# New places in the turn for the 37 kinds of pieces of a software-pipelined tokens stage

## The reference, cut to what matters

```python
x = conv_layer(x, ...)                     # 1x1 conv, depthwise 3x3, 1x1 conv, each with batchnorm; + x
t = to_tokens(x)                           # (32, 3136, 96)
def attn(v):
    h = relu(bn1(v @ w1.T))                # (32, 3136, 192)
    X = fft(h, axis=tokens, norm='ortho')
    xr = relu(X.real * rd - X.imag * idg + rb)
    xi = relu(X.imag * rd + X.real * idg + ib)
    y = ifft(xr + 1j * xi, axis=tokens, norm='ortho').real
    return bn2(y @ w2.T)                   # (32, 3136, 96)
t = t + attn(layernorm(t))                 # layernorm over the 96 channels of a token
t = t + ffn(layernorm(t))                  # 96 -> 384 -> relu -> 96, operands rounded to fp8, sums to fp16
return from_tokens(t)
```

## Time and profile before

| | us |
|---|---|
| median of 3 runs | 5966.26 |
| lowest, highest | 5946.19, 5976.29 |
| the profiled execution | 5949.41 |
| its span, first to last instruction | 5947.6 |
| PE busy over the span | 5426.3 (91%) |
| DVE busy | 3628.5 (61%) |
| ACT busy | 3418.6 (57%) |
| POOL busy | 1708.1 (29%) |

### The profile page before, as it was taken

How to read it: one execution, slowest core, us unless ns; L and a number is a source line. 1 busy time by engine, 2 the same in 40 slices (tenths; PEclk the granted TensorE clock), 3 DMA queues, 4 the chain that set the end, 5 groups by cost and what they waited for, 6 DMA issues and landing times.

```text
span 5947.6 us, 161991 instructions
## 1 busy us (share of the span) xinstructions
PE 5426.3 (91%) x59604; PEld 3538.5 (59%) x59604; DVE 3628.5 (61%) x6670; ACT 3418.6 (57%) x5674; POOL 1708.1 (29%) x964
## 2 busy tenths in 40 slices
PE   4979999999999969999868999999999999999996
PEld 4956565555555534444356666666667666666663
DVE  1046666666666643333327787777777778777775
ACT  2445555555555546666446666666666666666652
POOL 0047676667666600000011111111111111111100
PEclk9989999999999989999969999999989999889986
DMA  3646666666666579999846655655655665565551
GB/s 82 155 119 163 164 158 159 163 151 162 162 161 164 138 250 334 341 334 332 266 128 164 170 156 156 170 160 157 167 161 160 165 169 154 157 168 152 157 134 43
DMA packets 553255, 1042.04 MB, mean 175 GB/s; under 512 B 178512, under 2 KB 347280, under 8 KB 535888
## 3 DMA queue, kind: packets, MB, share of 16 engines
q1 hardware_dynamic: 552512, 1031.93, 62.6%
HBM read 552.39 MB, written 478.94 MB: 173 GB/s over the span
## 4 chain that ended last, share of the span: by engine, by line
PE 34%; issue 7%; DMA 3%; ACT 2%; DVE 2%; POOL 1%; SPq 1%; ACTq 0%; POOLq 0%; DVEq 0%
PE bank_w L1327 6%; PE bank_s L1336 4%; PE bank_x L1282 4%; PE bank_o L1307 3%; PE bank_l L1237 3%; PE bank_c L1290 3%; PE bank_c L1291 2%; PE bank_o L1318 2%; PE bank_c L1297 2%; POOL onat L1527 1%; PE bank_l L1264 1%; PE bank_x L1279 1%; DMA d<-c_scratch 1%; PE bank_l L1225 1%; ACT h L1400 1%
## 5 line engine op out<-in xcount | busy, mean ns | idle before, releaser
L718 POOL TENSOR_TENSOR hlo<-h,hhi 128x1682 f16<-128x1682 f32 x288 | 977.0, 3392 | 522.6 <-DVE hhi L749 522.6
L733 DVE BATCH_NORM_STATS2 stats<-z 128x392 f32 (+1 forms) x1152 | 597.0, 560 | 592.4 <-ACT z L670 553.6
L1519 POOL TENSOR_TENSOR y<-zin,x_tok 96x448 f32<-96x448 f32 x224 | 263.2, 1175 | 2207.2 <-ACT zin L1475 2160.2
L680 ACT ACTIVATE h<-c1ps,s 128x1512 f32<-128x1512 f32 x288 | 465.0, 1615 | 748.2 <-PE c1ps L596 748.2
L888 PE MATMUL pps<-z2m,w3T 128*96 128x392 f32 x2048 | 707.6, 499 | 13.9 <-ACT z2m L865 13.9
L617 PE MATMUL dwps<-hhi,taps 64*64 64x392 f16 x13824 | 699.1, 334 | 0.3 <-issue 0.3
L617 PE MATMUL dwps<-hlo,taps 64*64 64x392 f16 x13824 | 690.8, 330 | 2.6 <-issue 2.6
L865 ACT ACTIVATE z2m<-z2m,s 128x784 f32<-128x784 f32 x512 | 491.0, 1029 | 253.1 <-DMA z2m<-z_scratch 253.0
L1527 POOL TENSOR_TENSOR onat<-tb,o 96x448 f32<-96x448 f32 x224 | 242.7, 1084 | 1143.4 <-DVE o L1586 1143.4
L888 PEld LDWEIGHTS pps<-z2m,w3T 128*96 128x96 f32 x2048 | 324.8, 164 | 387.2 <-issue 367.6
L617 PEld LDWEIGHTS dwps<-hlo,taps 64*64 64x64 f16 x13824 | 408.4, 107 | 188.9 <-issue 8.7
(11 more groups left out here) (218 smaller groups left out, 10110.4 us busy)
## 6 DMA issues: line engine op xcount, KB each, us to landing
z_scratch<-z SPq DMA_DIRECT2D x1152, 196.0 KB, 3.2
z2m<-z_scratch SPq DMA_DIRECT2D x128, 1568.0 KB, 19.6
a_scratch<-a SPq DMA_DIRECT2D x224, 384.0 KB, 2.8
bt<-a_scratch SPq DMA_DIRECT2D x96, 672.0 KB, 8.1
c_scratch<-cc SPq DMA_DIRECT2D x128, 336.0 KB, 4.2
d<-c_scratch SPq DMA_DIRECT2D x128, 336.0 KB, 4.4
xa<-in_x_dram SPq DMA_DIRECT2D x32, 1176.0 KB, 7.3
xin<-in_x_dram SPq DMA_DIRECT2D x32, 1176.0 KB, 8.3
```

The lines of the kernel that those rows point to most:

```text
L680: nc.scalar.activation(to, src, ACT.Relu, bias=s1[:, 1, u:u + 1], scale=s1[:, 0, u:u + 1]).then_inc(h_ready, 1)
L718: nc.gpsimd.tensor_tensor(to, h, hi, ALU.subtract).then_inc(lo_ready, 1)
L733: nc.vector.bn_stats(stats[:, i, v, at:at + 6], z2[:, v % 3, g, r, :]).then_inc(s_stat, 1)
```

## The change

The numbers of all 37 kinds in `PLACES` are others; nothing else in the kernel differs. The same instructions are issued, on the same engines and with the same waits. Two of the kinds:

```diff
@@ PLACES
- 'act_square1': (1674, 1957),
+ 'act_square1': (1766, 1978),
...
- 'row1': (2046, 2236),
+ 'row1': (2068, 2780),
```

More of the change, by code:

```diff
@@ new lines @@
+PLACES = {'load_in': (5, 73, 274, 393, 625, 703, 857),
+ 'act_bn3': (295, 451, 587, 745, 869, 999, 1157),
+ 'pool_y': (310, 500, 630, 782, 793, 1013, 1331),
+ 'store_t': (1149,),
+ 'act_square1': (1766, 1978),
+ 'mean1': (1872, 1994),
+ 'square1': (1876, 2014),
+ 'act_mean1': (1903, 2063),
+ 'dve_var1': (2037, 2148),
+ 'act_std1': (2013, 2138),
+ 'row1': (2068, 2780),
+ 'w1': (2210, 2258, 2309, 2388, 2535, 2687, 2749, 2849, 2903, 3005, 3111, 3208, 3266, 3320),
+ 'dve_rstd1': (2224, 2271, 2288, 2419, 2610, 2693, 2781, 2901, 2969, 3025, 3152, 3232, 3305, 3356),
+ 'act_h': (2215, 2282, 2379, 2513, 2626, 2716, 2783, 2873, 2966, 3042, 3194, 3250, 3300, 3407),
+ 'stage1': (2271, 2399, 2548, 2585, 2757, 2852, 2875, 3023, 3147, 3214, 3300, 3368, 3432, 3527),
+ 'act_a': (2307, 2467, 2606, 2607, 2795, 2853, 2889, 3052, 3226, 3253, 3327, 3409, 3537, 3557),
+ 'store_a': (2355, 2449, 2951, 3118, 3342, 3519, 3543),
+ 'load_b': (3660, 3704, 3991, 4115),
+ 'spectrum': (3865, 3988, 4323, 4604, 4877, 5033),
+ 'act_scaled': (3893, 4062, 4402, 4708, 4942, 5110),
+ 'dve_real': (3937, 4127, 4453, 4755, 5000, 5332),
+ 'act_relu': (3958, 4133, 4520, 4777, 5003, 5379),
+ 'dve_fold': (4049, 4372, 4682, 4947, 5135, 5404),
+ 'w2': (4469, 4735, 4872, 5073, 5413, 5577, 5673, 5810),
+ 'dve_wz': (4513, 4757, 4913, 5127, 5458, 5586, 5722, 5821),
+ 'stage3': (4579, 4801, 4924, 5162, 5492, 5613, 5753, 5826),
+ 'dve_c': (4663, 4792, 5077, 5239, 5549, 5662, 5787, 5904),
+ 'store_c': (4733, 5139, 5636, 5859),
+ 'load_d': (4918, 5406, 5662, 6036),
+ 'load_t': (5414, 5443, 5569, 5623, 5829, 5893, 6173),
+ 'stage4': (6145, 6237, 6289, 6330, 6421, 6514, 6580),
+ 'dve_residual': (6221, 6262, 6295, 6376, 6469, 6558, 6655),
+ 'act_square2': (6460, 6673),
+ 'mean2': (6442, 6699),
+ 'square2': (6467, 6746),
+ 'act_mean2': (6505, 6770),
+ 'dve_var2': (6483, 6769),
+ 'act_std2': (6534, 6798),
+ 'dve_rstd2': (6561, 6843),
+ 'spread_mean': (6806, 7192, 7488, 7763),
+ 'spread_rstd': (6969, 7224, 7541, 7803),
+ 'dve_centre': (6800, 6902, 7222, 7225, 7516, 7529, 7783),
+ 'dve_norm': (7010, 7013, 7266, 7270, 7561, 7567, 7788),
+ 'mlp1': (7047, 7050, 7101, 7123, 7133, 7150, 7303, 7305, 7386, 7389, 7417, 7437, 7583, 7596, 7635, 7636, 7697, 7703,
+          7819, 7825, 7837),
+ 'act_h16': (7080, 7087, 7112, 7121, 7128, 7179, 7344, 7369, 7395, 7433, 7434, 7465, 7620, 7630, 7659, 7664, 7726,
+             7732, 7839, 7841, 7867),
+ 'dve_bias1': (7081, 7122, 7154, 7163, 7201, 7205, 7352, 7399, 7405, 7457, 7466, 7467, 7617, 7641, 7666, 7703, 7728,
+               7741, 7850, 7861, 7921),
+ 'dve_relu1': (7173, 7275, 7423, 7497, 7680, 7760, 7929),
+ 'mlp2': (7253, 7315, 7461, 7499, 7720, 7801, 7915),
+ 'act_o': (7289, 7359, 7487, 7540, 7751, 7787, 7957),
+ 'dve_bias2': (7325, 7380, 7553, 7556, 7772, 7841, 8107),
+ 'pool_out': (7618, 7663, 7815, 7860, 7941, 8081, 8299),
+ 'store_out': (8190,)}
```

## The result

The changed kernel takes 5989.2 us (median of 8 runs, 5980.1 to 6015.9); the kernel before, run beside it, 5964.6 us (8 runs, 5940.6 to 5976.3). The ratio is 1.0062, with a 95% interval of 1.0045 to 1.0079: slower, with the middle of the interval above the 0.5% that can be told from no change and its lower end just under it. The medians differ by 24.6 us. The interval of the ratio allows 27 to 47 us; its middle is 37 us, or 1.16 us a turn, where the prediction had 49.6 us and 1.55.

What follows compares the result with a forecast made beforehand. PE, busy for 91% of the span, was taken to set the pace. Terms (a) to (g) summed to 1.55 us a turn, 49.6 us over 32 turns, giving 6016 us on the 5966.3 median; 8-in-10 range 5930 to 6065.

Steps and rivals of the forecast that it cites:

- (a): First `square2`: `act_bn3[1]` put ahead of `act_square2[0]` makes PE wait, 0.4 us a turn.
- (b): Second `square2`: `w2[1]` ahead of `square2[1]` delays `dve_var2[1]`, `dve_rstd1[6]`, `act_h[6]` and PE's `w1[7]`, 0.25 us a turn.
- (c): Two norms ahead of `dve_rstd1[9]` delay `act_h[9]` and ACT's copy chain to `act_h16[2]`, 0.25 us a turn.
- (d): Last chunk: `dve_bias2[4]` ahead of `dve_centre[6]` delays `spread_rstd[3]` and `mlp1[18]`, 0.2 us a turn.
- (e): Turn's start: `act_square1[1]` ahead of `act_std1[0]` delays the deviations, their DMA and `w1[0]`, 0.5 us a turn.
- (f): Loop's jump: `mean1[1]`, now ahead of PE's jump, waits for `dve_var1[0]` behind DVE's; 0.3 us per jump, 0.15 a turn.
- (g): `store_c[3]` no longer waits behind `load_t[5]` on SP, shortening the first `stage4`'s wait: a gain, -0.2 us a turn.
- What else moves lies beside other work: Remaining moves, such as `row1[1]`, `act_bn3`, `pool_y`, next-image loads and `act_square1[0]`, were taken as covered and given no price.
- Swallowed: Rival, chance 0.25: ACT and DVE catch up, `load_d` covers (e), only (d) and (f) remain, 11 us: 5977, no change.
- Faster through `c_scratch`: Rival, chance 0.20: `store_c[3]` lands early enough that the first `stage4` never waits, 37.7 us go: 5928.
- More half clock: Rival, chance 0.12: idle time at the turn's start grows, rounds all go to 0.89, 34 us on top: 6050.

Runs made afterwards that it cites:

- e11: The kernel before with the exchanges of (a) and (b) alone: 5976.1 us, ratio 1.0044 to the kernel before.
- e10: The kernel before with one ACT exchange, `act_bn3[6]` moved behind `act_h16[5]`: 5938.1 us, ratio 0.9998 to the kernel before.
- e1: The changed kernel with `dve_centre[6]` ahead of `dve_bias2[4]` again, undoing (d): 5995.1 us, ratio 1.0063 to the kernel before.
- e12: The kernel before with the exchanges of (e) and (f) alone: 5991.9 us, ratio 1.0078 to the kernel before.
- e3: The changed kernel with the exchanges of (e) and (f) undone: 5977.9 us, ratio 1.0042 to the kernel before.
- e6: The kernel before with only SP's places taken from the changed kernel: 5966.9 us, ratio 1.0030 to the kernel before.
- e7: The changed kernel with SP's places as before and the exchanges of (a) to (f) undone: 5966.3 us, ratio 1.0031 to the kernel before.
- e9: The kernel of e7 with `dve_relu1[1]` and `act_square1[0]` also put back: 5949.1 us, ratio 1.0004 to the kernel before.
- e8: The kernel before profiled once more, with no edit: 5953.7 us in one run.
- e2: The changed kernel with the mid-turn exchanges of (a), (b) and (c) undone: 6008.4 us, ratio 1.0096 to the kernel before.

## Why the prediction came out as it did

The direction and the kind of cause were right: PE's order hardly changed, no large wait was taken away, and short waits appeared in PE's row at named places. The total was near, 49.6 us against 37. The working behind it was right in part only, and it left the clock out, which by the estimate above carries some 14 of the 37.

- **(a)** predicted 0.4, measured 0.22 us a turn, in the changed kernel and alone (e11). Right place, cause and row. The size is off since the 0.76 us of `act_bn3[1]` delayed the square by less than its length: it starts 0.77 us ahead of L1225 now and started 1.25 us ahead before, 0.48 us later against a slack of 0.33.
- **(b)** predicted 0.25, measured 0.31. Right, through the chain named.
- **(c)** predicted 0.25, measured -0.08 and +0.04, so nothing. This step failed: "the copy chain there has no slack" holds for PE behind `act_h16`, and e10 shows it, but the delay of `act_h[9]` did not reach that chain; that it ended in ACT's gaps is likely and not traced. I had bounded it by 0 and chose the wrong side.
- **(d)** predicted 0.2, measured 0.09; gone in e1.
- **(e) and (f)** predicted 0.65 together. Alone they cost 1.44 us a turn (e12), undone in the changed kernel they give back 0.2% (e3), 0.37 a turn. The mechanism of (f) is in the rows, and it was undersized: in e12 a jump costs 1.3 to 1.5 us more, 0.6 to 0.7 a turn, where I had 0.15. Of (e) the wait is in the rows, but its 0.5 us show in no stretch, as `load_d`'s wait shrinks beside it. The size depends on what else stands at the turn's start: PE there waits for the last of several chains (the transfer of `load_d`, the row DMA, DVE's variance), so removing the one that is last shows the next.
- **(g)** predicted -0.2 by `load_d` landing sooner. This failed. The wait did fall in the profile, but by no more than between two profiles of the same kernel; and SP's order alone makes the kernel slower by 0.3% (e6), not faster.
- **"What else moves lies beside other work"** failed for one or both of `dve_relu1[1]` and `act_square1[0]`, 0.27% together (e7 to e9). For the first the median stretch shows 0.14 us a turn; the second I had called free with the wrong picture of ACT's gaps, if it is the one. That the rest together is free is shown by e9.

The parts alone are worth 0.44% (e11), 0.78% (e12) and 0.30% (e6), 1.52% in all, and together 0.62%. So my sum was near by luck as well as by reading: terms too small at the turn's start, an overlooked pair, a clock left out, and an addition of costs that overlap.

**The rivals.** *Swallowed* was right for (c) alone. *Faster through `c_scratch`* is refuted: the wait persists and moves between profiles. *More half clock* priced the clock at 34 us on top of the sum, with rounds at a grant of 0.89; they came at 0.90 to 0.94. Its sign was right and its size too large. The Trainium skill, "TensorE: Matmul & The Clock Gate", section "HAM oscillation — how this bites in real kernels", has the work behind a wait of TensorE start cold. The rows agree that it is the work behind the turn's end that runs cold (six matmuls at L1207 take 1.72 us in the jump row of before and 0.95 in that of e12, both shown under e12), and the lower clock of the changed kernel's runs goes the way of that rule. That it must cost time they don't show: e8 had more of it than before for the same time.

**What stays open.** Why the clock falls in mid-turn in 11 or 12 of 24 turns of e2 and e12 and in 5 of the changed kernel, so whether a loss that the clock carries belongs to the moved piece; what in SP's order lowers the clock; and which of the last two pieces costs.

## What to carry to other kernels

Read the slack of each moved piece where the bounding engine is gapless and at full clock, and look at several turns to know that it is: there the sign, the chain and the size to some 0.2 us come out, and starts show delays that busy time and lists of waits hide under modelled ends. Where several chains meet, at a turn's start, costs neither add nor subtract; a part must be tried alone in the kernel before and undone in the changed one, and only both say what it is worth. Profile the kernel before a second time before reading anything from a sum of waits: here one such sum was 37.7 and 24.7 us in the same kernel. And set the granted clock of all runs side by side, as one profile can miss it: e6's loss shows there and in no stretch.

## What the runs showed of the hardware

- In mid-turn PE's pieces start at the same distances in every execution, to 0.01 or 0.02 us on the mean of 24 turns (6.35, 6.35, 6.35 us in before, e8 and e9), as long as the clock stays full.
- The clock falls to half in mid-turn too, with no long wait ahead of it: in before in 7 of 24 turns, each time with one wait of 0.47 us in PE's row in the 10 us ahead of the fall. The same matmuls then take 6.8 to 7.6 us and not 5.25.
- Kernels with the same instructions in another order differ in their mean granted clock beyond its scatter: 0.9280 in 23 runs of before, 0.9255 in 12 of e6.
- Around the turn's end the same kernel shows `spectrum[0]` at half clock in 18 or in 24 of 29 turns, with the whole turn at 88.00 and 88.05 us: there half clock cost nothing, as PE waits behind it either way.
- PE's wait at the loop's jump is 2.8 us on the mean in before (34.1 in 12) and 3.2 in the changed kernel (38.6 in 12), though the jump is the same; a wait for another engine ahead of it adds to it in full.
